# Block 1's self-attention: the query chunks of a pair of batches spread over two turns, the values' transpose after the weighing

## The reference

```python
def mha(xq, ctx, wq, wk, wv, wo, bo):
    q = (xq @ wq).reshape(b, sq, H, DH).transpose(0, 2, 1, 3)
    k = (ctx @ wk).reshape(b, sk, H, DH).transpose(0, 2, 1, 3)
    v = (ctx @ wv).reshape(b, sk, H, DH).transpose(0, 2, 1, 3)
    scores = jnp.einsum('bhqd,bhkd->bhqk', q, k) / math.sqrt(DH)
    attn = jax.nn.softmax(scores, axis=-1)
    out = jnp.einsum('bhqk,bhkd->bhqd', attn, v)
    return out.transpose(0, 2, 1, 3).reshape(b, sq, INNER) @ wo + bo
...
h1 = adaln(x, t, norm1_w, norm1_b)
x = mha(h1, h1, attn1_wq, attn1_wk, attn1_wv, attn1_wo, attn1_bo) + x
h2 = adaln(x, t, norm2_w, norm2_b)
x = mha(h2, context, attn2_wq, attn2_wk, attn2_wv, attn2_wo, attn2_bo) + x
```

## Time and profile before

| | |
|---|---|
| median of 3 runs | 6768.27 us (6766.1 to 6770.31) |
| profiled execution, its own time | 6758.11 us |
| its span, first to last instruction | 6756.3 us |
| mean granted TensorE clock | 0.941 of full speed |
| block 1's self-attention, first scores to the end of the last projection | 3742 to 3919 us |

### The profile page before, as it was taken

How to read it: one execution, slowest core, us unless ns; L and a number is a source line. 1 busy time by engine, 2 the same in 40 slices (tenths; PEclk the granted TensorE clock), 3 DMA queues, 4 the chain that set the end, 5 groups by cost and what they waited for, 6 DMA issues and landing times.

```text
span 6756.3 us, 141162 instructions
## 1 busy us (share of the span) xinstructions
PE 6176.6 (91%) x56181; PEld 4441.0 (66%) x56181; DVE 3931.5 (58%) x8705; ACT 3318.7 (49%) x6385; POOL 2240.2 (33%) x2179
## 2 busy tenths in 40 slices
PE   5799999999999999999979899999689999989998
PEld 4466666666666656666644777777457777766983
DVE  2677777777777777777755244444434444444553
ACT  1466656666566566665643234444223333333763
POOL 3555555555555555555520000000001111137440
PEclk6799999999999999999989799999789999998998
DMA  1566656656566566665730000000000000021000
GB/s 46 89 103 95 101 96 101 101 90 109 87 102 109 86 99 102 98 102 90 116 68 18 13 33 33 28 33 24 13 25 13 15 15 10 15 76 39 2 1 22
DMA packets 396487, 407.88 MB, mean 60 GB/s; under 512 B 125575, under 2 KB 372946, under 8 KB 393786
## 3 DMA queue, kind: packets, MB, share of 16 engines
q1 hardware_dynamic: 395834, 398.85, 33.3%
HBM read 158.00 MB, written 0.46 MB: 23 GB/s over the span
## 4 chain that ended last, share of the span: by engine, by line
PE 70%; DVE 9%; POOL 7%; issue 6%; ACT 4%; DMA 2%; SPq 1%; POOLq 1%; DVEq 0%; ACTq 0%
PE psum L2205 10%; PE psum L2172 9%; PE psum L1546 6%; PE psum L1534 6%; PE psum L1520 6%; PE psum L2217 4%; PE psum L1560 4%; PE psum L1568 3%; PE psum L1666 3%; POOL slot_context L3361 2%; DVE row_max L1885 2%; PE psum L435 2%; PE psum L421 2%; PE psum L1675 1%; DMA key_stack<-key_parts 1%
## 5 line engine op out<-in xcount | busy, mean ns | idle before, releaser
L1885 DVE TENSOR_REDUCE row_max<-psum 112x1 f32<-112x500 f32 x2304 | 1443.7, 669 | 282.8 <-PE psum L1534 277.7
L2003 ACT ACTIVATE weights<-psum 125x448 f32<-125x448 f32 x2304 | 1154.0, 544 | 764.0 <-PE psum L1520 749.7
L1520 PEld LDWEIGHTS psum<-query_stack,key_stack 121*125 121x125 bf16 x9216 | 829.0, 140 | 367.6 <-issue 165.7
L1534 PE MATMUL psum<-key_stack,query_stack 97*112 97x500 bf16 x2304 | 906.9, 394 | 102.8 <-DVE row_max L1885 81.9
L1520 PE MATMUL psum<-query_stack,key_stack 121*125 121x112 bf16 x9216 | 931.3, 224 | 70.1 <-ACT weights L2003 64.9
L2729 POOL TENSOR_TENSOR l_ctx_v<-l_ctx_v,l_ctx_w 125x512 f32<-125x512 f32 x48 | 60.9, 1269 | 2292.0 <-DVE l_ctx_v L2723 2292.0
L2205 PE MATMUL psum<-l_ctx_v,l_turned 125*128 125x128 f32 x5376 | 713.8, 281 | 16.0 <-ACT l_turned L2243 12.4
L2285 DVE TENSOR_REDUCE l_stat<-psum 128x1 f32<-128x1500 f32 (+1 forms) x224 | 391.7, 1748 | 573.4 <-PE psum L2172 573.4
L2205 PEld LDWEIGHTS psum<-l_ctx_v,l_turned 125*128 125x128 f32 x5376 | 643.3, 191 | 58.7 <-ACT l_turned L2243 40.0
L1546 PE MATMUL psum<-weights,values 125*17 125x112 f32 x18432 | 677.3, 265 | 0.2 <-ACT weights L2003 0.2
L1546 PEld LDWEIGHTS psum<-weights,values 125*17 125x17 f32 x18432 | 379.2, 97 | 263.1 <-ACT weights L2003 144.8
(11 more groups left out here) (526 smaller groups left out, 10283.8 us busy)
## 6 DMA issues: line engine op xcount, KB each, us to landing
key_stack<-key_parts SPq DMA_DIRECT2D x1728, 125.0 KB, 4.4
ctx_t<-in_ctxT SPq DMA_DIRECT2D x96, 750.0 KB
l_ctx_v<-in_ctxV SPq DMA_DIRECT2D x32, 750.0 KB
query_stack<-query_parts SPq DMA_DIRECT2D x576, 28.0 KB, 3.6
l_ctx_t<-in_ctxT SPq DMA_DIRECT2D x16, 750.0 KB
slot_context<-in_ctxV SPq DMA_DIRECT2D x16, 750.0 KB
key_stack<-ctx_mask_rows SPq DMA_DIRECT2D x576, 3.9 KB
sm_w<-in_sm_w SPq DMA_DIRECT2D x3, 2048.0 KB
```

The source lines that it names most:

```text
L1520: mm = e.matmul(self.k.psum[0:KN, h, (p % 4) * QC:(p % 4 + 1) * QC], ks[:, p, kt * KN:(kt + 1) * KN], q[:, p * QC:(p + 1) * QC])
L1534: e.matmul(self.k.psum[0:QC, 2 + n % 2, 0:500], q[0:ROWS_MAX, p * QC:(p + 1) * QC], ks[0:ROWS_MAX, p, c * 500:(c + 1) * 500]).then_inc(sel ...
L1885: e.tensor_reduce(self.largest[:, i % PAIRS, i // PAIRS:i // PAIRS + 1], k.psum[0:QC, 2 + i % 2, 0:500], AX.X, ALU.max, negate=True).then_ ...
L2003: e.activation(half(self.p[kt % 2], h), self.k.psum[0:KN, h, 0:HALF], ACT.Exp).then_inc(self.exped.sem, 1)
```

## The change

The four chunks of a pair are computed two by two in the two turns ahead of it: in turn i the chunks 2(i mod 2) and 2(i mod 2)+1 of pair i//2+1, the first (here: A) behind the scores, the second (B) behind the transposes of the weights. The values' transpose of batch i-2 moves behind the weighing of batch i-3, at the end of the turn. ACT's list takes the same order: A's copy, the exponential, the copies of the transposed weights, B's copy, its half of the weighed values, the values' copy. The order given to `side` is A, B, values in each turn.

```diff
--- before.py
+++ after.py
@@ -2457,11 +2457,15 @@
         self.ff_down = sig("mlp_down", 2)
         order = [("q", 0, g) for g in range(4)]
         for i in range(B + 2):
-            if i < B and i % 2 == 1 and i + 1 < B:
-                order += [("q", (i + 1) // 2, g) for g in range(4)]
+            order += [("q", *self.chunk_at(i, j)) for j in range(2) if self.chunk_at(i, j)]
             if i >= 2:
                 order.append(("v", i - 2))
         self.side = Banks(k, "side", [6], order)
+
+    def chunk_at(self, i, j):
+
+        pair = i // 2 + 1
+        return (pair, 2 * (i % 2) + j) if pair < BH else None
 
     def fetch_heads(self, e, n):
         for name, buf in zip("qkvo", self.by_head):
@@ -2517,14 +2521,12 @@
                     e.wait_ge(s.shifted.sem, s.shifted(i - 2))
                 q = self.q[i // 2 % 2][:, i % 2, :, :].rearrange("p h q -> p (h q)")
                 self_scores_tensor(e, k, s, i, q, k.xn)
-                if i % 2 == 1 and i + 1 < B:
-                    for g in range(4):
-                        self.chunk_tensor(e, (i + 1) // 2, g)
+            if self.chunk_at(i, 0):
+                self.chunk_tensor(e, *self.chunk_at(i, 0))
             if 0 <= i - 2 < B:
-                key = ("v", i - 2)
-                e.wait_ge(side.emptied(*key), side.before(*key))
-                e.transpose(side.bank(*key)[0:S, 0:128], of_batch(k.xn, i - 2), k.ident[:, :]).then_inc(side.filled, 1)
                 self_turn_tensor(e, k, s, buf, i - 2)
+            if self.chunk_at(i, 1):
+                self.chunk_tensor(e, *self.chunk_at(i, 1))
             if i >= 5 and i % 2 == 1:
                 pair = (i - 5) // 2
                 if pair:
@@ -2533,6 +2535,10 @@
             if 0 <= i - 3 < B:
                 e.wait_ge(side.emptied("v", i - 3), side.after("v", i - 3))
                 self_weigh_tensor(e, k, s, buf, i - 3)
+            if 0 <= i - 2 < B:
+                key = ("v", i - 2)
+                e.wait_ge(side.emptied(*key), side.before(*key))
+                e.transpose(side.bank(*key)[0:S, 0:128], of_batch(k.xn, i - 2), k.ident[:, :]).then_inc(side.filled, 1)
         e.wait_ge(self.z_self.sem, self.z_self(BH - 1))
         e.wait_ge(self.heads_arrived.sem, self.heads_arrived(1))
         self.folds.tensor(e, k, 2, self.by_head[0], self.by_head[1])
@@ -2568,22 +2574,24 @@
         for g in range(4):
             self.chunk_scalar(e, 0, g)
         for i in range(B + 4):
+            if self.chunk_at(i, 0):
+                self.chunk_scalar(e, *self.chunk_at(i, 0))
             if i < B:
-                if i % 2 == 1 and i + 1 < B:
-                    for g in range(4):
-                        self.chunk_scalar(e, (i + 1) // 2, g)
                 self_exp_scalar(e, k, s, buf, i)
+            if 0 <= i - 2 < B:
+                self_turn_scalar(e, k, s, buf, i - 2)
+            if self.chunk_at(i, 1):
+                self.chunk_scalar(e, *self.chunk_at(i, 1))
+            if 0 <= i - 3 < B:
+                if i >= 7 and i % 2 == 1:
+                    e.wait_ge(s.projected.sem, s.projected((i - 7) // 2))
+                self_gather(e, k, s, buf, i - 3, 0)
             if 0 <= i - 2 < B:
                 b = i - 2
                 e.wait_ge(side.filled, side.at("v", b))
                 if b >= 4:
                     e.wait_ge(s.weighed.sem, s.weighed(b - 4, 1))
                 e.activation(buf.v[b % 4], side.bank("v", b)[0:S, 0:128], ACT.Copy).then_inc(side.emptied("v", b), 1)
-                self_turn_scalar(e, k, s, buf, b)
-            if 0 <= i - 3 < B:
-                if i >= 7 and i % 2 == 1:
-                    e.wait_ge(s.projected.sem, s.projected((i - 7) // 2))
-                self_gather(e, k, s, buf, i - 3, 0)
         self.folds.scalar(e, k, 2, self.q_fold)
         self.folds.scalar(e, k, 3, self.o_fold)
         ln_scalar(e, k, LN_L1(1))
```

## The result

| | median, us | runs | ratio to before (95%) |
|---|---|---|---|
| before | 6768.27 | 5 (6764.4 to 6775.3) | |
| changed | 6731.41 | 5 (6729.2 to 6744.7) | 0.9949 (0.9938 to 0.9960) |

Forecast were 6749.3 us and a range of 6735 to 6758. The ratio's interval stands for a gain of 27 to 42 us.

A forecast was written before the change was run, and what follows sets the result against it. PE was taken to bound block 1's self-attention stage. Waits removed, 24.0 us, less 3.5 kept, 0.9 cover and borders, 0.6 tail: 19.0 us off the 6768.3 median gives 6749.3 us, range 6735 to 6758.

The forecast's parts named there:

- What one wait costs: PE's wait for ScalarE's `l_q` copy, start to start: 0.85 us at the high clock level, 0.87 at the low.
- the tail: Last turn: the weighing of batch 15 must wait for its values' copy; 0.6 us charged, bounds 0.3 and 0.9.
- Which waits stay: Turns 0, 1 and 2 keep four full waits at the low level, 3.5 us.
- The cover: Between A's and B's starts: A and the weights' transposes fill 1.69 of 1.78 us, up to 0.09 us wait.
- The charge of 0.9 us: Allowance for the thin cover and the added borders between kinds of matmul together; bounds 0 and 2.5 us.
- The other engines: ScalarE's reordered copies: exponentials put off by 0.2 us but with room; VectorE's program and DMA untouched.
- The sum: Self-attention stage: 24.0 us of waits less 3.5, 0.9 and 0.6 gives 19.0 us less.
- The clock: PE's clock rises at the same point of the work, the first projection, which comes about 7 us earlier.
- Rival 1: Denser order lifts PE's clock earlier, at 3770 us: 15.5 us more gain, 34.5 in all, 6734; chance 0.13.
- Rivals 2, 3 and 4: Handover uncovered, gain 8.7 us (0.13); clock misses rise, 23 us slower (0.04); later clock levels hide 6 us (0.03).

The follow-up runs named there:

- the early half: New order in turns 0 to 5 only (pairs 1 to 3), old order from turn 6 on, against the kernel before: 6736.2 us, ratio 0.9953.

## Why the prediction was wrong

- **What one wait costs** (0.85 us high, 0.87 us low): right. A pair shows 0.83, and 16 waits less the tail brought 12.7 us where 16 x 0.83 - 0.56 gives 12.7.
- **Which waits stay**: right, all four in their places (the last of them at the high level already). **The cover** of 1.69 us against 1.78: B starts 1.74 us after A, one wait of 0.2 us in all (turn 4, in both traces of the changed kernel). The charge of 0.9 us was somewhat high: all waits less the four kept ones were 20.5 us, and eight at 0.87 (reckoned) and sixteen at 0.83 (measured) are 20.2, so 0.3 us would have done.
- **The other engines**: right, no new wait of PE for the weights' copies. **The tail**: 0.56 us, 0.6 said.
- **The sum** of these terms was 19.0 us; the runs make it 20.2 - 0.56 = 19.7 us.
- **The clock**: this step failed: "So an unbroken PE did not lift it, a projection did", and from it "I let the clock rise at the same point of the work". The 18.2 us without a hole held scores, transposes and weighings, and one chunk, at the end. I took from it that closeness does not count, while it only showed that this mix does not suffice. And I asked what the waits do to the clock only in the high stretch, so I put their removal at nothing for the clock. The runs showed in its place: with the idle time between the chunks filled, by matmuls or by transposes, the clock rose 11.8 and 11.7 us after the first scores; with A, transposes and B in a row, after 21.6 to 22.3 us; with four chunks kept apart by waits, at the first projection. The rise 37 us of low-level work earlier (59 us after the first scores expected, 21.8 found) is worth 37 x 0.47 = 17.4 us (scores from start to start take 1.60 us at the high level and 3.02 at the low one: 3765.18 to 3768.20 above), and 19.7 + 17.4 = 37.1 us. The stage gives 37.1 and 37.2; that it fits to a tenth is chance, for the sum leaves out the 0.2 us wait, and 0.47 is taken from the scores alone.
- **Rival 1** was this case: rise at 3770, gain 34.5 us, 6734. It had 0.13. Its argument for ("chunks, the denser kind, now adjoin other work") was the right one, and the range should have gone beyond its time: its lower end, 6735, lay above this rival's 6734, though the text wants it "with its full gain and 2 us more", which is 6732. A chance of 0.13 was so left outside the range. Rivals 2, 3 and 4 did not happen: the chances of faster, same and slower rested on the waits and pointed the right way.

What stays open: which property of PE's work lifts the clock (no idle time between the chunks, their number in a stretch, or the kind of the other work), and why a chunk with transposes behind it lifts it in one execution and not in the next. Nor do I know why it fell in the last projection of some executions and not of others, or what made the 0.2 us wait in turn 4.

## What to carry to other kernels

Where a stage begins at the low clock level, ask first what ends it, and look at the kinds of matmuls that stood close together before it rose, not only at whether PE was busy: here the clock was worth nearly as much as all the waits (17.4 and 19.7 us). A short handover wait costs its idle time plus the laid-open end of the pipelined matmuls (here 0.63 us idle, 0.83 in all); take it start to start. And with one bank for two uses, put other work of PE between them that is as long as copy and drain together.

## What the runs showed of the hardware that I had not expected

- Needless work made the kernel faster: 0.86 us of it (at the low level) behind each of 8 chunks shortened the stage by 20.7 us, by the clock alone.
- Transposes counted as well as matmuls in this: rise 11.7 against 11.8 us after the first scores.
- Once up, the clock stayed up through 0.63 us waits: in the kernel before 16 of them, in the early half too (1.00 from 3766 to 3870 us). At the stage's end it fell in some executions and not in others of the same kernel (last projection 5.43 or 3.80 us before, 5.42 or 3.79 changed).
- Unchanged code ahead of the stage ended between 3742 and 3760 us in the traces, and medians of kernels with equal stages (156.0 and 156.1 us) lay 8.6 us apart; a stage is better judged by its own length in the trace.
